# A fused window-attention and mixture-of-experts block: sums, masks and a product on other engines, and new orders

## The reference

```
x = x + attention(LN(x))        # 7x7 windows of the image rolled by 3, 4 heads of 8 channels
x = x + experts(LN(x))          # per pixel: router softmax over 8 experts, the best 2

attention: p = softmax(q k^T)            # per window and head, 49 x 49
           p = p + bias(rel_table) + mask   # after the softmax, not before it
           out = (p v) w_proj + b_proj
experts:   out = sum over the 2 best e of share_e * (t W_e + b_e)
```

## Time and profile before

| what | value |
|---|---|
| runs (three), median | 822.0 us |
| the profiled execution's own time | 823.93 us |
| its span, first to last instruction | 822.1 us |
| PE busy, matmuls | 603.0 us (73%) |
| DVE busy | 585.8 us (71%) |
| ACT busy | 370.9 us (45%) |
| POOL busy | 355.3 us (43%) |
| mean granted clock of PE | 0.854 of full |
| DMA moved | 100.79 MB, 53.0% of 16 engines' span in SP's queue |
| chain that ended last | PE 48%, DVE 16%, ACT 12%, issue 12%, DMA 4%, POOL 4% |

### The profile page before, as it was taken

The page is one execution under the profiler, slowest core; times in us unless marked ns, Lnnn a source line. Parts: engine busy times, 40 slices in busy tenths (PEclk is TensorE's granted clock), DMA queues, the critical chain, the costliest instruction groups (busy, mean ns, idle before and its releaser), DMA issues.

```text
span 822.1 us, 28813 instructions
## 1 busy us (share of the span) xinstructions
PE 603.0 (73%) x12210; PEld 406.6 (49%) x12210; DVE 585.8 (71%) x878; ACT 370.9 (45%) x737; POOL 355.3 (43%) x458
## 2 busy tenths in 40 slices
PE   2688788878687886777778787868787886886314
PEld 1456655545465554545545554645555555563101
DVE  7356768868787776878777787888788774766613
ACT  1565645454636435463644546463545434331100
POOL 2536463534536163453716454453737356123110
PEclk9999977979989688999989899998899798856555
DMA  4101338294755718384573938484665719175963
GB/s 112 35 4 42 71 99 185 57 197 100 160 125 112 171 50 200 94 184 101 129 153 76 197 75 199 101 182 100 144 139 127 176 45 199 41 169 120 203 149 81
DMA packets 40511, 100.79 MB, mean 123 GB/s; under 512 B 12736, under 2 KB 14784, under 8 KB 38848
## 3 DMA queue, kind: packets, MB, share of 16 engines
q1 hardware_dynamic: 39952, 98.05, 53.0%
q10 hardware_dynamic: 432, 0.90, 0.3%
HBM read 58.78 MB, written 8.03 MB: 81 GB/s over the span
## 4 chain that ended last, share of the span: by engine, by line
PE 48%; DVE 16%; ACT 12%; issue 12%; DMA 4%; POOL 4%; SPq 2%; ACTq 0%; POOLq 0%; DVEq 0%
PE ps_pv L1296 9%; PE ps_acc L1372 6%; PE ps_win L1278 5%; PE ps_win L1249 5%; DVE mx L979 4%; PE ps_shared L1213 4%; PE ps_shared L1228 3%; DMA gates<-shares_kept 3%; PE ps_shared L1316 3%; ACT pt L824 3%; PE ps_win L1257 3%; DVE gates L1082 2%; ACT mr L814 2%; ACT vb L781 2%; DVE st L969 2%
## 5 line engine op out<-in xcount | busy, mean ns | idle before, releaser
L979 DVE TENSOR_REDUCE mx<-ps_win 128x32 f32<-128x1568 f32 x64 | 114.5, 1789 | 90.5 <-PE ps_win L1249 90.4
L1082 DVE TENSOR_TENSOR gates<-gates,x 128x1792 f32<-128x1792 f32 x64 | 115.3, 1839 | 50.9 <-DMA gates<-shares_kept 50.3
L1296 PEld LDWEIGHTS ps_pv<-vb,pt 128*49 128x49 f32 x4096 | 113.2, 138 | 46.5 <-issue 42.3
L1296 PE MATMUL ps_pv<-vb,pt 128*49 128x18 f32 x4096 | 119.9, 207 | 19.4 <-issue 11.7
L640 POOL TENSOR_TENSOR on<-on,obs 128x256 f32<-128x256 f32 x64 | 46.5, 728 | 186.1 <-DVE on L1006 170.2
L824 ACT ACTIVATE pt<-ps_win 128x784 f32<-128x784 f32 x128 | 98.4, 821 | 51.7 <-PE ps_win L1278 51.7
L1278 PE MATMUL ps_win<-qbd,kp 32*49 32x196 f32 x2048 | 82.9, 376 | 12.8 <-issue 12.8
L1249 PE MATMUL ps_win<-kbd,qp 32*49 32x196 f32 x2048 | 65.5, 360 | 27.9 <-ACT pt L824 21.3
L814 ACT COPY mr<-ps_win 128x512 bf16<-128x512 bf16 x64 | 37.5, 586 | 104.0 <-PE ps_win L1257 103.9
L632 POOL TENSOR_SCALAR qbd<-qp,const_tile 128x392 f32<-128x392 f32 x128 | 78.5, 625 | 0.0
L606 POOL TENSOR_TENSOR xc<-xc,st 112x896 f32<-112x896 f32 x16 | 27.1, 1697 | 118.1 <-DVE st L948 118.1
(11 more groups left out here) (95 smaller groups left out, 1140.7 us busy)
## 6 DMA issues: line engine op xcount, KB each, us to landing
gates<-shares_kept SPq DMA_DIRECT2D x128, 392.0 KB, 10.0
...
```

What stands on the lines that cost most here:

```text
L979: nc.vector.tensor_reduce(mx[g % 2].rearrange("n a x h -> n a (x h)"), ps_win[:, :, 0:8 * N].rearrange("n a (k m) -> n a k m", m=N), AX, A ...
L1082: nc.vector.tensor_tensor(gate, gate, x4[w.par][:, :, columns(half)], ALU.mult).then_inc(gated, 1)
L1296: ins = mm(ps_pv[PAD * x:PAD * x + N, c0:c0 + SLOT], pt[g % 2][:, x, place, h, :], vb[u.par][:, 2 * g + x, a, h, :], start=True, stop=True)
```

## The change

The diff does five things. The bias part is no longer added by POOL: `ot` on PE, which turned the sum by a transposition, now turns both parts as products with the identity that accumulate in PSUM, and the projection's bias is added by a product of a row of ones with the bias, ahead of the products of `y` in the same bank. Both halves of the key masks are made by ACT. The fourth gate product (high half of the experts, second part of the columns) is made by POOL. `replicate` becomes two entries of SP's list and `gates` three. And all lists are laid out anew. Cut to its core (the lists of ACT and `LAST`, changed throughout, are left out):

```diff
 FIRST = {
     "SP": [
-        ("load", 0, 0), ("keep", 0, 0), ("load", 1, 0), ("keep", 1, 0), ("load", 2, 0),
+        ("load", 0, 0), ("keep", 0, 0), ("load", 1, 0), ("keep", 1, 0),
...
     "DVE": [
-        ("norm1_center", 0, 0), ("place", 0, 0), ("norm1_scale", 0, 0), ("norm1_root", 0, 0), ("prepare", 0, 0),
+        ("place", 0, 0), ("norm1_center", 0, 0), ("norm1_scale", 0, 0), ("norm1_root", 0, 0), ("prepare", 0, 0),
+        ("norm1_center", 1, 0), ("maximum", 0, 0), ("norm1_scale", 1, 0), ("maximum", 0, 1), ("norm1_root", 1, 0),
     ],
...
 STEPS = {
     "SP": [
-        ("store", 0, -3), ("replicate", 0, -1), ("keep", 0, 2), ("load", 0, 3), ("gates", 0, -1),
+        ("load", 0, 2), ("gates", 1, -2), ("gates", 2, -2), ("replicate", 0, -1), ("store", 0, -3),
+        ("replicate", 1, -1), ("keep", 0, 2), ("gates", 0, -1),
     ],
     "POOL": [
-        ("norm1_center", 0, 1), ("pv", 1, -1), ("norm2_root", 0, -2), ("pv", 2, -1), ("place", 0, 0), ("pv", 3, -1),
-        ("kept", 0, -1), ("norm1_root", 0, 1), ("kmask", 1, 0), ("top2", 5, -2), ("norm2_center", 0, -1),
-        ("place", 1, 0), ("pv", 0, 0),
+        ("mul", 3, -2), ("norm1_root", 0, 2), ("top2", 5, -1), ("place", 1, 1), ("norm2_center", 0, 0),
+        ("norm1_center", 0, 3), ("norm2_root", 0, 0), ("place", 0, 2),
     ],
...
     "DVE": [
-        ("top2", 4, -3), ("pv", 0, -1), ("norm2_center", 0, -2), ("maximum", 2, -1), ("norm2_scale", 0, -2),
-        ("norm1_center", 0, 1), ("norm2_root", 0, -2), ("pv", 1, -1), ("maximum", 3, -1), ("pv", 2, -1),
-        ("norm1_scale", 0, 1), ("mul", 0, -3), ("mul", 1, -3), ("maximum", 0, 0), ("place", 0, 1), ("pv", 3, -1),
-        ("top2", 0, -2), ("mul", 2, -3), ("mul", 3, -3), ("top2", 1, -2), ("final", 0, -3), ("top2", 2, -2),
-        ("final", 1, -3), ("norm1_root", 0, 1), ("back", 0, -1), ("back", 1, -1), ("maximum", 1, 0), ("top2", 3, -2),
+        ("top2", 3, -2), ("top2", 4, -2), ("back", 1, -1), ("norm2_center", 0, -1), ("pv", 0, 0), ("maximum", 2, 0),
+        ("norm2_scale", 0, -1), ("pv", 1, 0), ("norm1_center", 0, 2), ("maximum", 3, 0), ("norm2_root", 0, -1),
+        ("pv", 2, 0), ("mul", 0, -2), ("maximum", 0, 1), ("mul", 1, -2), ("pv", 3, 0), ("mul", 2, -2),
+        ("norm1_scale", 0, 2), ("maximum", 1, 1), ("top2", 0, -1), ("top2", 1, -1), ("final", 0, -2),
+        ("top2", 2, -1), ("norm1_root", 0, 2), ("final", 1, -2), ("back", 0, 0), ("place", 0, 1),
     ],
     "PE": [
-        ("route", 0, -2), ("pv", 3, -1), ("logits", 0, -2), ("sum", 0, -3), ("shift", 0, 0), ("ot", 0, -1),
-        ("scores", 0, 0), ("ot", 1, -1), ("ob", 0, 0), ("sum", 1, -3), ("final", 0, -3), ("sum", 2, -3),
-        ("sum", 3, -3), ("final", 1, -3), ("y", 0, -1), ("y", 1, -1), ("maximum", 1, 0), ("xt", 0, 1), ("pv", 0, 0),
-        ("shift", 1, 0), ("scores", 1, 0), ("ob", 1, 0), ("xt", 1, 1), ("maximum", 2, 0), ("share", 0, -2),
-        ("k", 0, 1), ("pv", 1, 0), ("shift", 2, 0), ("scores", 2, 0), ("q", 0, 1), ("maximum", 3, 0), ("pv", 2, 0),
-        ("v", 0, 1), ("x2t", 0, -1), ("shift", 3, 0), ("scores", 3, 0), ("v", 1, 1), ("x2t", 1, -1),
-        ("maximum", 0, 1),
+        ("sum", 3, -3), ("pv", 0, 0), ("final", 1, -3), ("y", 0, -1), ("y", 1, -1), ("scores", 1, 0), ("ob", 1, 0),
+        ("xt", 0, 1), ("maximum", 2, 0), ("share", 0, -2), ("xt", 1, 1), ("pv", 1, 0), ("k", 0, 1), ("shift", 2, 0),
+        ("q", 0, 1), ("scores", 2, 0), ("maximum", 3, 0), ("pv", 2, 0), ("shift", 3, 0), ("scores", 3, 0),
+        ("v", 0, 1), ("maximum", 0, 1), ("x2t", 0, -1), ("x2t", 1, -1), ("pv", 3, 0), ("v", 1, 1), ("shift", 0, 1),
+        ("route", 0, -1), ("scores", 0, 1), ("sum", 0, -2), ("ot", 0, 0), ("logits", 0, -1), ("maximum", 1, 1),
+        ("sum", 1, -2), ("ot", 1, 0), ("sum", 2, -2), ("ob", 0, 1), ("shift", 1, 1), ("final", 0, -2),
     ],
 }
...
@@ -315,10 +312,11 @@
         w_proj_rows = part["w_proj"]
         wr = part["wr"]
         we = part["we"].rearrange("p (s c) -> p s c", s=2)
-        bp = part["bp"][0:ROWS, :]
+        bp = part["bp"][0:1, :]
         rel_raw = sb("rel_raw", [128, WS, WS, HEADS])
         bt = sb("bt", [128, HEADS, 4, PAD])
         plus_1_c = sb("plus_1_c", [ROWS, TOK])
+        one_row = sb("one_row", [1, ROWS])
         eps1, eps2, guess_scale = (sb(n, [ROWS, 1]) for n in ("eps1", "eps2", "guess_scale"))
 
...
-            def replicate(w, _):
-
-                sp.wait_ge(x2t_drained, upto("x2t_drained", w))
-                if w.has_before(2):
-                    sp.wait_ge(gated, upto("gated", w.before(2)))
+            def replicate(w, i):
+
                 x4p = x4[w.par]
-                for a in range(A):
-                    sp.dma_start(x4p[0:C, a, :], x2t[C * a:C * a + C, :]).then_inc(x4_first, 16)
-                sp.wait_ge(x4_first, upto("x4_first", w))
-                for e in range(1, 4):
-                    sp.dma_start(x4p[C * e:C * e + C, :, :].rearrange("p a t -> p (a t)"),
-                                 x4p[0:C, :, :].rearrange("p a t -> p (a t)")).then_inc(x4_ready, 16)
-
-            def gate_rows(w, _):
-
-                sp.wait_ge(shares_drained, upto("shares_drained", w))
-                if w.has_before(1):
-                    sp.wait_ge(gates_low, upto("gates_low", w.before(1)))
-                    sp.wait_ge(gates_high, upto("gates_high", w.before(1)))
-                for b in range(4):
-                    sp.dma_start(shares_kept[:, BLOCK * b:BLOCK * b + BLOCK],
-                                 shares[32 * b:32 * b + 32, :]).then_inc(shares_stored, 16)
+                if i == 0:
+                    sp.wait_ge(x2t_drained, upto("x2t_drained", w))
+                    if w.has_before(2):
+                        sp.wait_ge(gated, upto("gated", w.before(2)))
+                        sp.wait_ge(gated_pool, upto("gated_pool", w.before(2)))
+                    for a in range(A):
+                        sp.dma_start(x4p[0:C, a, :], x2t[C * a:C * a + C, :]).then_inc(x4_first, 16)
+                else:
+                    sp.wait_ge(x4_first, upto("x4_first", w))
+                    for e in range(1, 4):
+                        sp.dma_start(x4p[C * e:C * e + C, :, :].rearrange("p a t -> p (a t)"),
+                                     x4p[0:C, :, :].rearrange("p a t -> p (a t)")).then_inc(x4_ready, 16)
+
+            def gate_rows(w, i):
+
+                if i == 0:
+                    sp.wait_ge(shares_drained, upto("shares_drained", w))
+                    if w.has_before(1):
+                        sp.wait_ge(gates_low, upto("gates_low", w.before(1)))
+                        sp.wait_ge(gates_high, upto("gates_high", w.before(1)))
+                    for b in range(4):
+                        sp.dma_start(shares_kept[:, BLOCK * b:BLOCK * b + BLOCK],
+                                     shares[32 * b:32 * b + 32, :]).then_inc(shares_stored, 16)
+                    return
                 sp.wait_ge(shares_stored, upto("shares_stored", w))
                 if w.has_before(1):
                     sp.wait_ge(mixed, upto("mixed", w.before(1)))
-                for eh in range(2):
-                    for e in range(4):
-                        rows = bass.AP(shares_kept.tensor, shares_kept.offset + (4 * eh + e) * COLS,
-                                       [[0, C], [E * COLS, A], [1, COLS]])
-                        sp.dma_start(gates[C * e:C * e + C, eh, :, :], rows).then_inc(gates_high if eh else gates_low, 16)
+                eh = i - 1
+                for e in range(4):
+                    rows = bass.AP(shares_kept.tensor, shares_kept.offset + (4 * eh + e) * COLS,
+                                   [[0, C], [E * COLS, A], [1, COLS]])
+                    sp.dma_start(gates[C * e:C * e + C, eh, :, :], rows).then_inc(gates_high if eh else gates_low, 16)
...
-            def pv(u, g):
-
...
-            def kmask(v, i):
...
-            def kept(v, _):
...
+            def mul(w, _):
+
+                pool.wait_ge(x4_ready, upto("x4_ready", w))
+                pool.wait_ge(gates_high, upto("gates_high", w))
+                gate = gates[:, 1, :, columns(1)]
+                nc.gpsimd.tensor_tensor(gate, gate, x4[w.par][:, :, columns(1)], ALU.mult).then_inc(gated_pool, 1)
 
...
-                    act.wait_ge(o_ready, upto("o_ready", v.before(2)))
+                    act.wait_ge(ot_filled, upto("ot_filled", v.before(2)))
...
-                elif step == "kmask" and i == 0:
+                elif step == "kmask":
...
-                    dve.wait_ge(kept_biased, upto("kept_biased", w))
+                    dve.wait_ge(x_kept_ready, upto("x_kept_ready", w))
...
-                    if g:
-                        pe.wait_ge(k_masked_pool, upto("k_masked_pool", u))
-                    else:
-                        pe.wait_ge(k_masked, upto("k_masked", u))
+                    pe.wait_ge(k_masked, upto("k_masked", u, g // 2))
...
             def ot_turn(u, i):
 
                 shared_free("ot", u, i)
```

(23 more changed lines are left out.)

108 lines of the change are left out of this document (44 added, 64 removed), and 26 rows, old and new, of tables (LAST, STEPS).

## The result

The changed kernel takes 863.15 us (median of 4 runs, 860.16 to 866.98); the kernel before took 821.27 beside it. The ratio is 1.0509, with a 95% interval of 1.0444 to 1.0574: slower by 42 us. The forecast was 838. The medians in the table of the experiments take in every run; two of a_extra_c's four were slow, over 1.5% above its fastest, and the other two took 920.8 and 924.7.

The account below looks back on a forecast made before the run. No engine was full; a chain through several, paced by DVE's row maxima, bound the kernel. 823.9 profiled, +11 for twelve units, +2.5 at the start, +2 at the end gave 839.4, or 838 us as median; range 824 to 852.

Parts of the forecast that it names:

- C: Stretch from group 1's row maximum to group 2's, with turns and output step moved in: 16.3 us after the change.
- head: Start of the kernel: DVE clears the second value buffer before the first mean instead of after it, +2.5 us.
- PE's stall: PE stopping inside a scores step, released only by "issue", read as waiting for instructions while gate rows fill DMA queues: 3.9 us.
- A: Stretch from group 2's row maximum to group 0's of the next unit: 20.9 us by PE, 18.9 by the gate rows.
- B: Stretch from group 0's row maximum to group 1's: 9.3 us summed, 10.5 taken to allow for a slow PE clock.
- Bias sums on PE: Turns as eight products (2.3 us each) plus the projection's bias row (1.8) give PE about 5.1 us more per unit.
- rival 4: PE becomes the bound and all 5.1 us per unit show: +61, 888 us; chance 0.07.
- Product 3: Fourth gate product, moved from DVE to POOL: takes 2.5 us there, costed at nothing.
- Rival 3: DVE's and POOL's gate products block each other on one port, delaying DVE: about +2 us per unit, 862 us; chance 0.11.
- Masks: Key masks on ACT: four more activations, 2.18 us, costed at nothing; without cover at most 2.2.
- Rival 1: PE's instruction stall hides behind the gate rows' DMA: 18.9 us from group 2 to 0, 814 us in all; chance 0.32.
- Tail: End of the kernel: turns and output steps with a slow PE, +2 us, between -6 and +7.

Follow-up runs that it names:

- a_extra_c: The changed kernel with the bias row of the output step issued twice, in the stretch from group 1 to 2; 929.7 us, ratio 1.136.
- b_no_bias: The kernel before with both bias sums left out (neither on POOL nor on PE), orders as before; 804.8 us, ratio 0.981.
- a_no_bias: The changed kernel without PE's bias products (turns by transposition, no bias row; both biases missing from the output); 802.6 us, ratio 0.979.
- a_extra_gap: The changed kernel with two extra PE products (512 and 384 columns) ahead of group 3's maxima; 870.9 us, ratio 1.062.
- a_pool_bias: The changed kernel with both bias sums back on POOL as five adds per unit; 813.1 us, ratio 0.993.
- a_pool_place: The kernel of a_pool_bias with DVE's clearing of the second value buffer behind the first mean again; 803.3 us, ratio 0.983.
- a_kmask_pool: The changed kernel with the second half of the key masks back on POOL; 866.2 us, ratio 1.064.

## Why the prediction was wrong

The sign held, and so did the price of the products and of C; the size failed, 16 us forecast against 42. Two steps failed. The head has a term for the clearing alone, 2.5 us, and took 13.9. In the steady part the sum puts PE's stall into A, at 3.9; the runs show the stops in B, where the sum has no term for them, and A ends by another path.

- *Bias sums on PE*: the turns came out at 1.98 (2.3 predicted), the row at 1.86 (1.8). All of it was in the sum, as it should be. By the runs the products cost 4.25 us per unit in twelve units (5.1 predicted), and their total of 60.5 is the price that rival 4 gave, 61. But rival 4 started from 822; without POOL's adds the start is 805. The prediction put those adds at nothing, as work that "no maximum waited for"; b_no_bias shows 16 us.
- *The step that failed in the steady part is the run in B*, "9.3 ... I take 10.5". It is 11.9. Without the bias products it should have been 10.5 - 1.6 = 8.9 and is 10.7, so 1.8 us per unit were missing before anything was added; the turn's smaller cost gave 0.4 back. The profile shows where: in ten of the twelve units PE stops in B for 0.2 us or more with nothing but "issue" named, 17.8 us in all and 1.5 per unit (9.6 us in six units before, 20.5 in a_no_bias). Then it often runs at half clock, for which I had allowed 1.2. One such run; the window line gives PE's granted clock of its slow part, 0.51:
```profile
445.55 0.27 PE L1248 MATMUL ps_win<-mr,const_bf_tile 32*49 32x196 bf16 x3 [0.21 <-ACT mr L793]
447.19 0.36 PE L1248 MATMUL ps_win<-mr,const_bf_tile 32*49 32x196 bf16 x5 [1.38 <-issue]
...
448.06 0.99 PE L1254 MATMUL ps_win<-qbd,kp 32*49 32x196 f32 x16
448.97 1.72 PE L1358 MATMUL ps_acc<-gates,folded_tile 128*32 128x448 f32 x8
450.62 0.49 PE L1284 MATMUL ps_shared<-const_tile,on 128*128 128x128 f32 x2
```
```profile
447.19:450.62 3.43, 3.43 (x53) 1.35 (x53) 3.02 (x2) 1.51 (x2) 3.32 (x1) 0.51 0.32 80
```
The scores took 3.4 us instead of 1.12, the expert sum 1.65 instead of 0.9.
- *C*: 16.3 predicted, 16.1 measured; right, and PE-bound as worked out.
- *A*: 20.9 predicted, 20.7 measured, and that these agree is luck. The sum had A end by PE, with the stall of 3.9, and the gate rows 1.8 us earlier. But between group 3 and 0 PE stops for "issue" in one of the twelve units, 1.5 us (28.6 us in eleven units before), though the gate rows fill the DMA engines as they did (share 1.02 in the window above). So the reading that these rows cause the stall is not borne out; what causes it is open. The scores of group 3 in the unit shown, at half clock and without a stop:
```profile
434.59 0.38 PE L1248 MATMUL ps_win<-mr,const_bf_tile 32*49 32x196 bf16 x8 [0.68 <-ACT mr L793]
434.75 0.87 PE L1254 MATMUL ps_win<-qbd,kp 32*49 32x196 f32 x16
435.40 0.39 PE L1248 MATMUL ps_win<-mr,const_bf_tile 32*49 32x196 bf16 x8
435.57 0.98 PE L1254 MATMUL ps_win<-qbd,kp 32*49 32x196 f32 x16
...
438.36 1.58 PE L1225 MATMUL ps_win<-kbd,qp 32*49 32x196 f32 x32
```
What ends A in nine of the twelve units is product 0: group 0's reduction starts at its end, 0.5 to 3.1 us after PE's maxima have ended. In the unit shown the gate rows leave 7.9 after group 2's maximum (7.2 predicted) and need 11.66 from issue to product (9.73), so the product starts at 440.09, when PE's maxima have just ended. Group 2 to 3 took 10.2 instead of 9.0 for two reasons: the shares' store takes 2.83 instead of 1.70, so the load lands later, and POOL's centring holds up the shift's second half (1.76 instead of 0.30 us at 422.60, and much the same in ten of the twelve units).
- *Head*, the largest miss: 2.5 predicted, 13.9 measured. By the times to unit 3 the bias products are 5.4 of it (146.8 against 141.4 in a_no_bias), the new orders 10.6 (141.4 against 130.8 in b_no_bias), of which the clearing is 3.2 (shown), and POOL's adds give 2.1 back. a_extra_gap, the same up to there, needed 148.7, so these parts are good to some 2 us. None but the clearing was a term: the long PE run stands between group 1 and 2 while the pipeline fills too (37.0 us over the first three units instead of 26.5, and 4.2 back from group 0 to 1). Unit 0 takes 37.3 instead of 30.6, units 1 and 2 together 78.3 instead of 74.0. In unit 0 PE was granted 0.50 from 36 to 50 us; in a_no_bias, by the times of its steps, it was slow only to 43, and the unit took 33.0. The same step (64 products of scores and values) in the changed kernel and in a_no_bias:
```profile
42.94 2.86 PE L1272 MATMUL ps_pv<-vb,pt 128*49 128x18 f32 x64
```
```profile
43.00 1.65 PE L1272 MATMUL ps_pv<-vb,pt 128*49 128x18 f32 x64
```
The products are not the reason for that difference: the first turn stands at 73.07, behind unit 0. Two kernels without them took 37 us there (a_pool_bias, a_pool_place), and a_kmask_pool, which has them, took 33.0. What sets the clock there is open.
- *Product 3*: 2.5 predicted, 4.60 on average; it starts 0.05 behind DVE's product and is the one that waits. Rival 3 is right on the block and wrong on who pays. *Masks*: nothing, as predicted.
- *Rival 1* had the path of A right for nine units, group 0 right behind product 0, and its price wrong: the gate rows leave and land later than the sum had it, so A is 20.7 and not 18.9, and the stops went to B. *Tail*: 5.3 against +2, within its bounds.
